# Routed linear layer: halves of the expert products signalled singly, products ahead of the selection, the loop written out

## What is computed

```
def _L1_ffn_ref(x, tile_sigs, W, b):
    scores = jnp.einsum('bsd,td->bst', x, jnp.sign(tile_sigs))
    idx = jnp.argmax(scores, axis=-1)
    all_out = jnp.einsum('bsd,tde->bste', x, W) + b[None, None]
    out = jnp.take_along_axis(all_out, idx[:, :, None, None], axis=2)
    return out[:, :, 0, :]
...
x = x + _L1_ffn_ref(_layernorm(x, axis=-1), L1_ffn_tile_sigs, L1_ffn_W, L1_ffn_b)
```

## Time and profile before

| | us |
|---|---|
| median of 3 runs | 1026.29 |
| lowest and highest | 1025.15, 1029.08 |
| profiled execution, its own time | 1024.24 |
| its span, first to last instruction | 1022.5 |
| busy in the span: PE, DVE, ACT, POOL | 823.2, 746.9, 562.1, 204.5 |
| mean granted clock of TensorE | 0.912 |

### The profile page before, as it was taken

The page is one execution under the profiler, slowest core; times in us unless marked ns, Lnnn a source line. Parts: engine busy times, 40 slices in busy tenths (PEclk is TensorE's granted clock), DMA queues, the critical chain, the costliest instruction groups (busy, mean ns, idle before and its releaser), DMA issues. The chain is left out here.

```text
span 1022.5 us, 26783 instructions
## 1 busy us (share of the span) xinstructions
PE 823.2 (81%) x9567; PEld 490.9 (48%) x9567; DVE 746.9 (73%) x2473; ACT 562.1 (55%) x1398; POOL 204.5 (20%) x217
## 2 busy tenths in 40 slices
PE   5899999995975788696663397896986999999686
PEld 2577777774322233242131275563664555555343
DVE  5688888884389999999996795456463667767757
ACT  3788898886675658575240476453343333333244
POOL 1467766663000000000000011002210000000136
PEclk9999999998897788898797598997897999999889
DMA  7111111100000000000000903100570000000001
GB/s 241 33 44 43 40 37 41 41 6 2 1 0 0 1 1 0 1 1 0 1 0 8 166 2 117 52 5 19 205 274 1 1 1 0 0 0 1 1 11 31
DMA packets 23157, 36.54 MB, mean 36 GB/s; under 512 B 5668, under 2 KB 19748, under 8 KB 20644
## 3 DMA queue, kind: packets, MB, share of 16 engines
q1 hardware_dynamic: 23080, 35.53, 11.6%
HBM read 34.48 MB, written 1.05 MB: 35 GB/s over the span
## 5 line engine op out<-in xcount | busy, mean ns | idle before, releaser
L381 ACT ACTIVATE xa_prob<-xa_s,xa_nmax 128x257 f32<-128x257 f32 x256 | 128.1, 503 | 21.6 <-DVE xa_nmax L466 19.8
L568 POOL TENSOR_TENSOR xa_prob<-xa_prob,xa_rinv 128x1028 f32<-128x1028 f32 x64 | 121.5, 1900 | 75.8 <-DVE xa_rinv L473 74.6
L466 DVE CUSTOM_DVE_ANT_0 xa_s<-xa_s_ps,xa_nbias 128x257 f32<-128x257 f32 x256 | 93.2, 420 | 12.3 <-ACT xa_prob L381 6.4
L1492 POOL TENSOR_TENSOR mo_disp_t<-mo_disp_t,mo_rst 128x256 f32<-128x256 f32 x16 | 9.9, 616 | 377.0 <-DVE mo_rst L1472 377.0
L2117 PEld LDWEIGHTS ca_z_ps<-ca_xn_t,ca_m_t 128*128 128x128 f32 x512 | 62.0, 198 | 30.5 <-issue 26.0
L2200 ACT COPY ca_z<-ca_z_ps 128x512 f32<-128x512 f32 x64 | 37.5, 585 | 69.0 <-PE ca_z_ps L2117 69.0
L242 PE MATMUL xa_t_ps<-identity,xa_prob 128*128 128x128 f32 x512 | 69.4, 279 | 3.7 <-ACT xa_p_t L390 2.1
L2117 PE MATMUL ca_z_ps<-ca_xn_t,ca_m_t 128*128 128x128 f32 x512 | 67.9, 288 | 4.1 <-ACT ca_xn_t L2194 3.9
L456 DVE COPY xa_kvs<-xa_kv_ps 128x512 f32<-128x512 f32 x64 | 44.1, 689 | 34.5 <-PE xa_kv_ps L216 34.5
L242 PEld LDWEIGHTS xa_t_ps<-identity,xa_prob 128*128 128x128 f32 x512 | 54.8, 141 | 25.3 <-issue 25.3
L390 ACT COPY xa_p_t<-xa_t_ps 128x1024 f32<-128x1024 f32 x64 | 63.4, 990 | 2.7 <-PE xa_t_ps L242 2.7
(11 more groups left out here) (327 smaller groups left out, 1929.1 us busy)
## 6 DMA issues: line engine op xcount, KB each, us to landing
xa_ctx_t<-in_ctx_t SPq DMA_DIRECT2D x64, 128.5 KB, 2.1
room<-in_ctx_t SPq DMA_DIRECT2D x8, 1028.0 KB, 6.6
room<-in_ctx_n SPq DMA_DIRECT2D x8, 1024.0 KB, 4.8
ss_wx<-in_ss_wx SPq DMA_DIRECT2D x1, 2048.0 KB, 7.8
xres<-in_x SPq DMA_DIRECT2D x4, 256.0 KB, 5.5
out_x<-xres SPq DMA_DIRECT2D x4, 256.0 KB, 2.3
ma_mask_u<-in_mask SPq DMA_DIRECT2D x4, 128.5 KB
room<-in_ca_wk SPq DMA_DIRECT2D x1, 512.0 KB, 4.9
```

The costliest lines, as they stand in the source:

```text
L381: nc.scalar.activation(prob[:, r, g, :], s_sb[:, b, g, :], ACT.Exp, bias=nmax[:, r, g:g + 1], scale=-1.0, accum_out=rsum[:, r, g:g + 1]).t ...
L466: nc.vector.tensor_tensor_reduce(out=s_sb[:, b, g, :], in0=s_ps[:, g, 0:S], in1=nbias[:, g, :], scale=1.0, scalar=3e38, op0=ALU.add, op1=A ...
L568: nc.gpsimd.tensor_tensor(prob[:, r, :, :], prob[:, r, :, :], bc(rinv[:, r, :].rearrange("p (g o) -> p g o", o=1), (P, G, S)), ALU.mult).t ...
```

## The change

- On TensorE the scores of group q-1 stand behind the turn of group q, and those of the last group behind those.
- The products of tiles 0 and 1 are ahead of the wait for `hot`, and the stationary operand is `xn_t` itself: `lhs` and its copies on ScalarE are gone.
- Each half of a tile's products has its own signal (`low_mm`, `high_mm`) and its own waits: the low half waits for VectorE's work of tile t-2, the high half for ScalarE's. The bias product is a piece of its own (`own_bias`, signal `b_mm`), and in the loop it stands ahead of the products of tile t+2.
- ScalarE copies the bias product to `own`; VectorE adds it there and no longer reads `x_ps`. Its work on a tile is four operations where it was five.
- The multiplication of the bias table goes from POOL to VectorE, behind the normalisation.
- The loops are written out for all 16 tiles on all engines.

```diff
@@ routed_linear: TensorE
-            for t in range(T):
-                pe.wait_ge(xt_ready, t // 4 + 1)
-                nc.tensor.matmul(s_ps[:, t * E:t * E + E], xn_t[:, t, :], sigs[:, :], start=True, stop=True).then_inc(s_mm, 1)
...
-            def experts(t, j):
-                pe.wait_ge(lhs_ready, t + 1)
-                if later(t, 1):
-                    pe.wait_ge(acc_ready, STEPS * (t - 1))
-                    pe.wait_ge(part_ready, HALF * (t - 1))
-                for q in range(2):
-                    nc.tensor.matmul(y_ps[:, j, q, :], lhs[:, j, :], w[:, HALF * q:HALF * q + HALF, :], start=True, stop=True)
-                nc.tensor.matmul(x_ps[:, j, 0:D], hot_t[:, :], tile_at(bias, t), start=True, stop=True).then_inc(y_mm, 1)
...
+            def experts(t):
+                if t >= 2:
+                    pe.wait_ge(acc_ready, 2 * t - 2)
+                    pe.wait_ge(low_ready, 2 * t - 2)
+                nc.tensor.matmul(y_ps[:, t % 2, 0, :], xn_t[:, t, :], w[:, 0:HALF, :], start=True, stop=True).then_inc(low_mm, 1)
+                if t >= 2:
+                    pe.wait_ge(part_ready, HALF * (t - 1))
+                nc.tensor.matmul(y_ps[:, t % 2, 1, :], xn_t[:, t, :], w[:, HALF:E, :], start=True, stop=True).then_inc(high_mm, 1)
+
+            def own_bias(t):
+                if t >= 2:
+                    pe.wait_ge(own_ready, t - 1)
+                nc.tensor.matmul(x_ps[:, t % 2, 0:D], hot_t[:, :], bias[:, t, :], start=True, stop=True).then_inc(b_mm, 1)
+
+            for q in range(GROUPS):
+                turn(q)
...
+                if q >= 1:
+                    scores(q - 1)
+            scores(GROUPS - 1)
+            experts(0)
+            experts(1)
             pe.wait_ge(hot_ready, 1)
...
+            for t in range(T):
+                own_bias(t)
+                if t + 2 < T:
+                    experts(t + 2)
@@ routed_linear: ScalarE
+            for t in range(T):
+                act.wait_ge(b_mm, t + 1)
+                if t >= 2:
+                    act.wait_ge(low_ready, 2 * t - 3)
+                nc.scalar.copy(own[:, t % 2, :], x_ps[:, t % 2, 0:D]).then_inc(own_ready, 1)
+                act.wait_ge(high_mm, t + 1)
+                if t >= 2:
                     act.wait_ge(out_ready, t - 1)
                 for e in range(HALF):
...
@@ routed_linear: VectorE
+            nc.vector.tensor_tensor(bias[:, :, :], bc(bias_rep[:, :].unsqueeze(1), (P, T, D)),
+                                    bc(t_own[:, :].unsqueeze(2), (P, T, D)), ALU.mult).then_inc(bias_ready, 1)
...
+            def low_half(t):
+                j = t % 2
+                dve.wait_ge(low_mm, t + 1)
+                if t >= 2:
                     dve.wait_ge(out_ready, t - 1)
...
+                chosen(t, 0, acc[:, j, :], xres[:, t, :]).then_inc(acc_ready, 1)
+                dve.wait_ge(own_ready, t + 1)
+                chosen(t, 2, part[:, j, HALF, :], own[:, j, :]).then_inc(low_ready, 1)
+                dve.wait_ge(acc_ready, 2 * t + 1)
+                chosen(t, 1, acc[:, j, :], acc[:, j, :]).then_inc(acc_ready, 1)
+                dve.wait_ge(low_ready, 2 * t + 1)
+                chosen(t, 3, part[:, j, HALF, :], part[:, j, HALF, :]).then_inc(low_ready, 1)
...
+            for t in range(T):
+                low_half(t)
+                if t >= 1:
+                    finish(t - 1)
+            finish(T - 1)
```

More of the change, by code:

```diff
@@ L2333, in _, with scores @@
                     pe.wait_ge(xt_ready, q - 1)
[L2334 to L2335 removed]
+                for i in range(QT):
+                    last = nc.tensor.transpose(x_ps[:, q % 2, i * P:i * P + P], xn[:, QT * q + i, :], ident[:, :])
                 last.then_inc(xt_mm, 1)
[L2337 to L2340 removed]
+            def scores(q):
+                pe.wait_ge(xt_ready, q + 1)
+                for t in range(QT * q, QT * q + QT):
+                    last = nc.tensor.matmul(s_ps[:, t * E:t * E + E], xn_t[:, t, :], sigs[:, :], start=True, stop=True)
+                last.then_inc(s_mm, 1)
+            def experts(t):
[10 more added lines that the diff above has]
+                nc.tensor.matmul(x_ps[:, t % 2, 0:D], hot_t[:, :], bias[:, t, :], start=True, stop=True).then_inc(b_mm, 1)
+            for q in range(GROUPS):
+                turn(q)
+                if q == 1:
+                    pe.wait_ge(sign_ready, 1)
+                if q >= 1:
[3 more added lines that the diff above has]
+            experts(1)
             pe.wait_ge(hot_ready, 1)
@@ L2416, in _ @@
             dve.wait_ge(hot_ready, 1)
-            def add(t, j):
-                dve.wait_ge(y_mm, t + 1)
-                if later(t, 1):
-                    dve.wait_ge(out_ready, t - 1)
-                def times_hot(dst, e, first, count):
-                    if not first:
-                        dve.wait_ge(acc_ready, STEPS * t + count)
-                    dve.sem_inc(past_v, 1)
-                    y, hot_e = y_ps[:, j, 0, e * D:e * D + D], tile_at(hot, t)[:, e:e + 1]
-                    if first:
-                        nc.vector.tensor_scalar(dst, y, hot_e, None, ALU.mult).then_inc(acc_ready, 1)
-                    else:
-                        nc.vector.scalar_tensor_tensor(dst, y, hot_e, dst, ALU.mult, ALU.add).then_inc(acc_ready, 1)
-                nc.vector.tensor_tensor(acc[:, j, :], tile_at(xres, t), x_ps[:, j, 0:D], ALU.add).then_inc(acc_ready, 1)
-                times_hot(part[:, j, HALF, :], 2, True, 0)
-                times_hot(acc[:, j, :], 0, False, 1)
-                times_hot(part[:, j, HALF, :], 3, False, 2)
-                times_hot(acc[:, j, :], 1, False, 3)
@@ L2439, in finish, with chosen @@
-            def finish(t, j):
-                dve.wait_ge(sum_ready, 3 * (t + 1))
-                dve.wait_ge(acc_ready, STEPS * (t + 1))
-                nc.vector.tensor_tensor(tile_at(xres, t), acc[:, j, :], part[:, j, 0, :], ALU.add).then_inc(out_ready, 1)
-            def slot(t, j):
-                add(t, j)
-                if later(t):
-                    finish(t - 1, 1 - j)
-            slots(dve, slot, 0)
-            finish(T - 1, 1)
+            def chosen(t, e, dst, plus):
+                return nc.vector.scalar_tensor_tensor(dst, y_ps[:, t % 2, 0, e * D:e * D + D], hot[:, t, e:e + 1], plus, ALU.mult, ALU.add)
@@ L2451, in _, with finish @@
+            def finish(t):
+                dve.wait_ge(sum_ready, 3 * t + 3)
+                dve.wait_ge(acc_ready, 2 * t + 2)
+                nc.vector.tensor_tensor(xres[:, t, :], acc[:, t % 2, :], part[:, t % 2, 0, :], ALU.add).then_inc(out_ready, 1)
+            for t in range(T):
[3 more added lines that the diff above has]
+            finish(T - 1)
         @block.gpsimd
         def _(pool):
-            pool.wait_ge(w_ld, W_LD)
-            nc.gpsimd.tensor_tensor(bias[:, :, :], bc(bias_rep[:, :].unsqueeze(1), (P, T, D)),
-                                    bc(t_own[:, :].unsqueeze(2), (P, T, D)), ALU.mult).then_inc(bias_ready, 1)
@@ L2457, in sums @@
-            def sums(t, j):
-                pool.wait_ge(part_ready, HALF * (t + 1))
+            for t in range(T):
+                j = t % 2
+                pool.wait_ge(part_ready, HALF * t + HALF)
                 nc.gpsimd.tensor_tensor(part[:, j, 0:2, :], part[:, j, 0:2, :], part[:, j, 2:4, :], ALU.add).then_inc(sum_ready, 1)
@@ L2463, in sums @@
                 pool.wait_ge(sum_ready, 3 * t + 2)
-                pool.wait_ge(acc_ready, STEPS * t + 4)
+                pool.wait_ge(low_ready, 2 * t + 2)
                 nc.gpsimd.tensor_tensor(part[:, j, 0, :], part[:, j, 0, :], part[:, j, HALF, :], ALU.add).then_inc(sum_ready, 1)
-            sums(0, 0)
-            sums(1, 1)
-            with pool.Fori(1, T // 2) as i:
-                for j in range(2):
-                    sums(i * 2 + j, j)
 def statistics(nc, dve, t, xres, mv, stats, moments, res_ready, st_ready, mo_ready, past):
```

58 lines of the change are left out of this document (17 added, 41 removed).

## The result

The changed kernel is slower: 1042.1 us median of 4 runs (1040.37 to 1045.43), against 1025.72 us (4 runs, 1023.85 to 1029.08) for the kernel before. The ratio is 1.015, 95% interval 1.0118 to 1.0181: a loss clear of the noise, though a small one. The profiled execution took 1040.37 us with a span of 1038.5 us, against 1024.24 and 1022.5.

The account below looks back on a forecast made before the run. VectorE's loop, 2.26 us per tile, was taken to set the pace behind a serial head. Tile 2 starting 2.5 us sooner and 16.6 us more after it gave +14.1, on the median 1026.29: 1040 us, range 1035.5 to 1050.

Parts of the forecast that it names:

- The ring: Loop: bias product, copy, VectorE and next products wait on each other serially, 3.53 us per tile against 2.26 before; 71%.
- `nmr`: Head of the stage: moving the bias table's product off POOL frees this scale, 2.869 to 0.175 us, -2.69 us.
- Scores between turns: Head, TensorE: a quarter of the scores (0.94 us) after each turn fills gaps; gain 0.76 us, bounds 0 and 0.93.
- Products ahead of the selection: Head, TensorE: two tiles' products from 971.8 end at 976.9, between full clock (3.44 us) and half clock (6.86).
- Tile 2's start: Start of the loop: tile 2's low half at 979.5 against 981.98, 2.5 us sooner; what follows 16.6 us longer.
- The signals of the halves: Loop: the low half's own signal saves nothing, since the wait is for `own`.
- The written-out loop: Loop: takes VectorE's register work away, but VectorE no longer sets the pace, so gains nothing.
- Tail: End of stage: from tile 15's low half at 1025.4, POOL sums tile 15 until 1032.95, finish at 1033.3.
- The falling clock, first rival: Loop, TensorE: clock drops to half; four or five such turns give 1049 us, all thirteen 1065; 21%.
- The other side: Loop: ring not closed, POOL paces at 1.97 us per tile, total 1020 us; faster under 2.45 us; 4%.
- A turn much shorter than its parts: Loop: links overlap, turn near 2.8 us, total within 0.5% of before; 4%.

Follow-up runs that it names:

- e1: Changed kernel with bias product t+1 ahead of the products of tile t+2 on TensorE; 1018.88 us, ratio to before 0.9912.
- e5: Changed kernel with ScalarE copying each bias product once more into an unread buffer; 1047.32 us, ratio to before 1.0186.
- e6: Changed kernel with one more 128x128 addition per tile on POOL into an unread buffer; 1042.32 us, ratio to before 1.0138.
- e11: Kernel before with only the bias table's multiplication moved to VectorE; 1025.30 us, ratio to before 0.9984.
- e2: Changed kernel with the bias table's multiplication back on POOL; 1045.38 us, ratio to before 1.0181.
- e8: e1 plus 20 unused transposes of the identity on TensorE ahead of the first turn; 1016.87 us, ratio to before 0.9884.
- e10: Changed kernel with the halves' waits joined again on TensorE and VectorE; 1046.28 us, ratio to before 1.0192.
- e4: Changed kernel with the products of tiles 0 and 1 behind the transpose of hot; 1046.46 us, ratio to before 1.0178.
- e12: Kernel before with only this stage's loops written out for all 16 tiles; 1023.84 us, ratio to before 0.9978.
- e3: Changed kernel with all scores behind all turns, as in the kernel before; 1042.46 us, ratio to before 1.0158.

## Why the prediction was right, and where it was off

Forecast: 1040 us, 14.1 us more than before; measured 1042.1, which is 16.4 us more by the medians, 15.4 by the ratio and 16.7 in the stage. The mechanism was the forecast one, and e1, e5 and e6 show it. One term was wrong by 3.4 us; that the stage is off by 2.6 and not by more is luck, since errors the other way took 0.8 back.

- **The ring.** 3.53 us from rows, 3.525 in the trace (13 turns in 45.83 us, 981.97 to 1027.80): bias product to copy 0.42, VectorE's three operations 0.86, 0.15 to TensorE, 1.79 until the next bias product. The hand-over from ScalarE to VectorE, for which no row stood, was set at 0.05: copy to operation is 0.30 (984.19 to 984.49) against 0.27 + 0.05. That the chain closes through TensorE's order is shown by e1, that the copy is a link by e5, and that POOL is none by e6; the other links are read from the trace, where each is released by the one before it.
- **`nmr`.** -2.69 forecast; the selection moves by 2.70 us in e11 and by 2.77 in e2.
- **Scores between turns.** This term was wrong. Forecast: selection 8.7 us after L90 (971.8 - 963.1), measured 12.05. The step that failed is the price of a pass of scores, taken from the earlier trace rows as 0.94 us for a group. That row stood at full clock, as the trace of the kernel before has it (columns as above):

```profile
971.50:974.80 3.30, 3.30 (x32) 3.30 (x31) 0.00 (x0) 0.58 (x1) 0.00 (x0) 1.00 0.00 0
```

Between the turns the clock was half, and 8 passes took 1.7 us (16 of them 3.42): 2.9 us more for all the scores than the 3.76 forecast. The other 0.5 us are the turns: 0.72 us was taken for one, the span of its loads, while a turn takes 0.89 us before the next piece starts (967.74 to 968.63). The forecast weighed the clock for the wide products and the loop but not for the scores, which stand between them. e8 gives the same order at full clock: 7.68.
- **Products ahead of the selection.** They took 5.2 us (974.35 to 979.51), the middle of 3.44 and 6.86, for the plain reason that one tile had the half clock and one the full. In other executions of the same head they took up to 6.25 us (e10), so that the middle was hit is luck. e4 shows a gain of 1.9 us.
- **Tile 2's start.** The sum compares 979.5 with 981.98, but 981.98 is where tile 1's products start in the earlier trace rows; tile 2's start 1.94 us later:

```profile
983.92 1.88 PE L2352 MATMUL rl_y_ps<-rl_w,rl_lhs 128*128 128x512 f32 x4
```

The total does not change, its two halves do: forecast by the right row, tile 2 starts 4.4 us sooner and what follows is 18.5 us longer. Measured from L90, it starts 1.3 us sooner (19.48 against 20.79) and what follows is 18.0 us longer.
- **The signals of the halves.** Forecast to save nothing; 0.14 us per tile by e10. The forecast 3.53 us are the ring with the signals; without them a turn is 3.66 us.
- **The written-out loop.** Forecast at nothing here, since VectorE no longer paces. e12 shows 2.9 us in the kernel before; in the changed kernel VectorE waits 2.0 us per tile for `own`, so that it is hidden there is likely, but no run puts the loops back.
- **Tail.** From the low half of tile 15 to the last `xres` 7.45 us, forecast 7.9: POOL does its sums of the last two tiles in 3.52 us (1031.40 to 1034.92) where 3.80 was forecast, and begins 0.15 us sooner.

The scores' term made the selection 3.4 us later than forecast; the way from it to the first bias product (5.6 us where 6.0 was forecast) and the shorter tail gave 0.8 back: 72.76 against 70.2 forecast for the stage, or +16.7 where +14.1 was forecast.

- **The falling clock, first rival.** In the loop of the changed kernel it did not happen: granted clock 1.00 over 46 us with TensorE busy for 62% of it. In e3 and e10 it happened for one tile, behind the first standstill, and cost some 1.5 to 1.8 us. The Trainium skill's rule of a clock that swings between matmul groups ("TensorE: Matmul & The Clock Gate", section "A second HAM failure mode: psum-queue depth-cycling") would have given 1049 us and more; this trace's loop, 1.00 throughout, speaks against it here.
- **The other side.** It decided at a turn under 2.45 us; e1, with the ring open, has 1.97 us and is faster than before, as that rival's arithmetic said (20.3 us less than with the ring, 20.8 measured in the stage). The rival was priced rightly and did not apply. Its 1.97 us was POOL's 1.87 and 0.1, though, while in e1 TensorE's 1.94 us paces: the price was right because the two engines lie so close.
- **A turn much shorter than its parts.** Ruled out by the loop of the changed kernel: the links do not overlap, they add up to the 3.53 us.

With the ring opened, the other parts add up to a gain: e1 is 4.1 us shorter than before in the stage, and e8, with its twenty transposes, 9.4 us. But two of the parts alone, the bias table on VectorE (e11) and the loops written out (e12), gave 2.9 us each on the kernel before. Should they add up, the kernel before with both would take 50.3 us for the stage, less than e1; that is an estimate from two traces, and no run has the pair. Of the rest, the products ahead of the selection (e4) and, in the closed ring, the single signals (e10) show a gain in a trace; ScalarE's copy of the bias product was not tried alone.

## What to carry to other kernels

When a piece of work is split off and given its own place in an in-order list, draw the ring: who waits for its result, what that one releases, and whether the released instruction stands ahead of the next such piece in the same list. If it does, one round cannot overlap with the next, and a piece that is small and early to be had belongs ahead of the long ones. By the waits in the code, a third buffer would open this ring as well, as long as the products stay two tiles ahead; that was not tried. And price short matmuls at the clock that the stretch will have, not at the clock of the row they are read from: where a stage starts behind a standstill, cheap work to fill it on TensorE (e8, selection 4.4 us sooner) did more here than either order of the scores.

## What the hardware showed that was not expected

- A pass of scores (128 columns of weights loaded, 8 columns moved) takes 0.21 us at the granted clock of 0.50 (16 in 3.42 us) and 0.12 at 1.00 (16 in 1.90 us, e8): even where hardly a column is moved, the time nearly doubles at half clock.
- In e1 `finish` takes 0.80 us when it starts 0.08 us behind one of POOL's additions and 0.28 when it starts between them (986.75 and 988.69); the first ends 0.16 us after POOL's addition does. `nmr` in the earlier trace rows is the same picture. The Trainium skill, "SBUF — State Buffer", section "SBUF: two separate sides", says that a VectorE operation with two SBUF inputs and a GpSimd operation that reads SBUF take turns at a shared pair of ports, the later one blocked for the whole of the other's instruction; both places agree. In e12 it falls on the other side: POOL's addition takes 0.90 us instead of 0.72 where a `finish` of 0.28 us starts 0.03 us behind it (993.25 and 993.28). It costs e1 little, since TensorE's own 1.94 us leaves 0.03 of the 1.97.
- Ahead of the turns TensorE stands still for some 4 us, and the granted clock falls from 1.00 to 0.50: in the changed kernel it was still 0.99 from 961.0 to 964.1 and 0.50 from the first turn on, in e1 0.50 already from 961.8 to 965.9. Twenty transposes whose result nobody uses, put into that standstill, kept it at 1.00 through turns and scores; the selection came 4.4 us sooner (12.05 to 7.68, one trace each). It then fell to half in e8 without a standstill, behind the scores (0.53 from 970.8 to 974, TensorE busy for all 3.20 us).
